# Operand loads for the last feed-forward step moved to the head of each tile and onto ScalarE's DMA queue

## The reference

```python
def _L0_attn_ref(x, Wk, bk, Wv, bv, Wq, bq):
    k = jnp.fft.fft(x @ Wk.T + bk)
    v = jnp.fft.fft(x @ Wv.T + bv)
    q = jnp.fft.fft(x @ Wq.T + bq)
    kv = jnp.cumsum(k * v, axis=1)
    queried = kv * jnp.conj(q)
    nrm = jnp.sqrt(jnp.sum(jnp.abs(queried) ** 2, axis=-1, keepdims=True))
    queried = queried / (1e-09 + nrm)
    return jnp.real(jnp.fft.ifft(queried)) / np.sqrt(d)

def _L0_ffn_ref(x, k0, k1, k2, s0, s1, s2):        # weights are booleans, +1 or -1
    h = jnp.concatenate([x, -x], axis=-1)
    h = jax.nn.relu(s0 * _conn_dense(k0, h)) * 2    # 2048 -> 4096
    h = jax.nn.relu(s1 * _conn_dense(k1, h)) * 2    # 4096 -> 4096
    return s2 * _conn_dense(k2, h)                  # 4096 -> 1024

xn = _layernorm(x)                                  # x: (4, 8192, 1024)
x = x + _L0_attn_ref(xn, ...) + _L0_ffn_ref(xn, ...)
```

## Time and profile before

| | |
|---|---|
| Time before, median of 2 runs | 4163.52 us |
| The two runs | 4025.52 and 4301.52 us |
| Profiled execution, its own time | 4029.55 us |
| Its span on the slowest core (core 7) | 4026.0 us |
| Spans of the eight cores | 4003.2 to 4026.0 us |
| Busy share of the span: PE, DVE, ACT, POOL | 91%, 28%, 28%, 17% |

### The profile page before, as it was taken

One profiled execution on the slowest core, in us unless ns is written; L12 is line 12 of the kernel. 1 busy time (PEld: TensorE's weight loads), 2 busy tenths in 40 slices (PEclk: granted clock), 3 DMA queues, 4 the chain that ended last, 5 costly groups with the idle time before them and its releaser, 6 DMA issues.

```text
span 4026.0 us, 43761 instructions; the slowest of 8 cores (4003.2 to 4026.0 us)
## 1 busy us (share of the span) xinstructions
PE 3647.3 (91%) x16512; PEld 1590.1 (39%) x16512; DVE 1118.4 (28%) x1586; ACT 1131.1 (28%) x1504; POOL 698.7 (17%) x843
## 2 busy tenths in 40 slices
PE   4667896998994999999899999999989999999998
PEld 1323332333332444444344344444434444444443
DVE  0044446876860112011111201111121111112112
ACT  4744542555562110311311131031112103112110
POOL 0022224554640001001000100100010020011001
PEclk9778898999997999999999999999999999999999
DMA  4143346334315345234344523433343442344344
GB/s 84 21 105 84 86 98 105 68 82 97 63 48 162 136 153 178 88 147 149 115 155 154 170 94 148 148 122 148 147 157 115 151 152 105 148 148 134 126 157 136
DMA packets 331229, 491.52 MB, mean 122 GB/s; under 512 B 217360, under 2 KB 219408, under 8 KB 297232
## 3 DMA queue, kind: packets, MB, share of 16 engines
q0 software_dynamic: 97904, 377.53, 28.5%
q1 hardware_dynamic: 223504, 82.90, 8.9%
q10 hardware_dynamic: 9616, 28.32, 2.0%
HBM read 276.87 MB, written 58.72 MB: 83 GB/s over the span
## 4 chain that ended last, share of the span: by engine, by line
PE 82%; DMA 5%; DVE 4%; issue 3%; ACT 3%; SPq 2%; POOL 0%; DVEq 0%; ACTq 0%; POOLq 0%
PE pd L966 44%; PE pd L661 13%; PE pd L922 11%; PE pd L1037 10%; PE pd L666 2%; PE pd L297 2%; DMA xn_f<-xn_dram 1%; SPq L533 1%; DMA w2ring<-k2u 1%; SPq L900 1%; DMA wtmp<-Wk 1%; DVE bx_t L1066 1%; PE pd L504 1%; DVE xn_t L482 1%; DMA xn_dram<-xn_t 1%
## 5 line engine op out<-in xcount | busy, mean ns | idle before, releaser
L966 PE MATMUL pd<-r_t,w1r 128*128 128x512 bf16 x8192 | 1769.4, 379 | 7.8 <-ACT r_t L936 7.8
L966 PEld LDWEIGHTS pd<-r_t,w1r 128*128 128x128 bf16 x8192 | 801.0, 98 | 976.2 <-issue 11.5
L984 DVE TENSOR_SCALAR w1r<-w1r 128x4096 bf16<-128x4096 bf16 x232 | 284.7, 1227 | 1810.3 <-DMA w1r<-w1s 1810.3
L922 PE MATMUL pd<-xn_f,K0d_t 128*128 128x512 bf16 x2048 | 459.1, 388 | 109.9 <-DVE bx_t L1070 55.9
L992 ACT ACTIVATE r_t<-pd,s_scales 128x512 bf16<-128x512 f32 x256 | 175.9, 687 | 1112.5 <-PE pd L966 1111.8
L979 POOL DMA_DIRECT2D w1r<-w1s x232 | 123.7, 533 | 2083.6 <-PE pd L966 2053.4
L1037 PE MATMUL pd<-w2ring,r_t 128*128 128x512 bf16 x2048 | 445.5, 379 | 14.3 <-ACT r_t L992 7.8
L922 PEld LDWEIGHTS pd<-xn_f,K0d_t 128*128 128x128 bf16 x2048 | 203.7, 100 | 365.4 <-issue 134.6
L1037 PEld LDWEIGHTS pd<-w2ring,r_t 128*128 128x128 bf16 x2048 | 198.8, 98 | 261.0 <-issue 25.7
L936 ACT ACT_TABLE_LOAD x64 | 82.1, 1283 | 588.0 <-PE pd L922 519.4
L1053 DVE TENSOR_SCALAR w2ring<-w2ring 128x1024 bf16<-128x1024 bf16 x224 | 95.8, 428 | 436.9 <-DMA w2ring<-k2u 436.9
(11 more groups left out here) (151 smaller groups left out, 2484.4 us busy)
## 6 DMA issues: line engine op xcount, KB each, us to landing
w1r<-w1s POOLq DMA_DIRECT2D x256, 1024.0 KB, 4.6
w2ring<-k2u POOLq DMA_DIRECT2D x256, 256.0 KB, 2.7
conv_t<-k0u POOLq DMA_DIRECT2D x64, 256.0 KB, 3.9
w1s<-k1u SPq DMA_DIRECT2D x32, 512.0 KB, 5.9
bx_t<-x_own SPq DMA_DIRECT2D x32, 512.0 KB, 4.7
out<-bx_t ACTq DMA_DIRECT2D x32, 512.0 KB, 3.3
x_t<-x_extra POOLq DMA_DIRECT2D x8, 1024.0 KB, 10.4
k0s<-conv_o SPq DMA_DIRECT2D x32, 256.0 KB, 2.6
```

Source lines behind the costliest of these rows:

```text
L922: inst = te.matmul(reg.ap, K0d_t[:, dk * F0 + m * 128: dk * F0 + (m + 1) * 128], xn_f[fb][:, dk * TST:(dk + 1) * TST], start=(dk == 0), st ...
L966: inst = te.matmul(reg.ap, w1ring[c % 3][:, k * 128:(k + 1) * 128], r0_t[:, k * TST:(k + 1) * TST], start=(k == 0), stop=(k == NF0 - 1))
L984: lambda: v.tensor_scalar(w1ring[c % 3][:], w1ring[c % 3][:], 2.0, -1.0, op0=OP.mult, op1=OP.add))
```

## The change

In `emit_compute_b` the four loads of `part_t` and the four of `bx_t` are emitted at the head of the tile, ahead of the first layer, and not between the second and third layers. The `bx_t` loads go from SP's list to ScalarE's. Buffers, sizes and numbers of transfers stay as they were. The edit in the loop of part A leaves out an `if` whose two branches were the same.

```diff
@@ -807,10 +807,7 @@
-        if it < NST:
-            emit_next_xload()
-        else:
-            emit_next_xload()
+        emit_next_xload()
@@ -907,6 +904,17 @@
     def emit_compute_b(j, fkeys):
         fb = j % 2
+        for tci in range(NTC):
+            @block.scalar
+            def _(sc, j=j, tci=tci):
+                dstep(sc, "act", s_pr[tci], [f"partial_dram{tci}"], [f"bpart{tci}"],
+                      lambda: sc.dma_start(
+                          part_t[tci][:],
+                          partial_dram.ap()[j * TST + tci * 128: j * TST + (tci + 1) * 128, :]))
+                dstep(sc, "act", s_bx[tci], [], [f"bx{tci}"],
+                      lambda: sc.dma_start(
+                          bx_t[tci][:],
+                          x_own.ap()[j * TST + tci * 128: j * TST + (tci + 1) * 128, :]))
@@ -994,21 +1002,6 @@
-        for tci in range(NTC):
-            @block.scalar
-            def _(sc, j=j, tci=tci):
-                dstep(sc, "act", s_pr[tci], [f"partial_dram{tci}"], [f"bpart{tci}"],
-                      ...
-
-            @block.sync
-            def _(sync, j=j, tci=tci):
-                dstep(sync, "sp", s_bx[tci], [], [f"bx{tci}"],
-                      ...
```

More of the change, by code:

```diff
@@ L996, in emit_compute_b @@
         r1keys = [f"r1_{c}" for c in range(NF1)]
-        for tci in range(NTC):
-            @block.scalar
-            def _(sc, j=j, tci=tci):
-                dstep(sc, "act", s_pr[tci], [f"partial_dram{tci}"], [f"bpart{tci}"],
-                      lambda: sc.dma_start(
-                          part_t[tci][:],
-                          partial_dram.ap()[j * TST + tci * 128: j * TST + (tci + 1) * 128, :]))
-            @block.sync
-            def _(sync, j=j, tci=tci):
-                dstep(sync, "sp", s_bx[tci], [], [f"bx{tci}"],
-                      lambda: sync.dma_start(
-                          bx_t[tci][:],
-                          x_own.ap()[j * TST + tci * 128: j * TST + (tci + 1) * 128, :]))
         for c in range(4):
```

## The result

| | |
|---|---|
| Ratio to before | 1.0033, 95% interval 1.002 to 1.0045 |
| Profiled execution's span, slowest core | 4035.7 us (4019.2 to 4035.7) |
| Median of 17 runs | 4040.95 us (4034.34 to 4615.12) |
| Kernel before, all 16 runs | 4080.82 us (4022.62 to 4663.73) |

The change costs 0.33%, some 13 us, where 7 us were forecast.

A forecast was written before the change was run, and what follows sets the result against it. The prediction took TensorE, busy 91% of the span, to bound the kernel. It summed 4029.55 + 5 (start) + 2 (seven borders) + 0 = 4036.5 us, with a range of 4018 to 4175.

The forecast's parts named there:

- the upper bound of a gain: All of TensorE's waits for w2ring together, 6.4 us, as the most the change could win; taken as 0.
- The term for the start of part B: Eight loads, 3 MB, issued at about 1217 beside the transposes that TensorE waits for: a cost of 5 us.
- sharing about half and half: Start of part B: moved loads partly ahead of the transposes, partly in the slack after 1254; 5 us, between 0 and 9.
- The upper bound of 9 us: Start of part B: the cost if 3.1 MB go wholly ahead of the transposes at 349 GB/s.
- The term for the seven borders: ScalarE's eight issues and four store-landing waits ahead of the first relu: 2 us for seven borders, kept between 0 and 20.
- the supply by issue time: Borders: eight issues behind the fourth store end at S + 6.6, the first region comes free at S + 8.6: cost 0.
- S: The start of a tile's first matmul, from which the prediction counts times at a border.
- two supply times: When ScalarE frees the first region at a border: S + 8.6 by issue time; S + 8.6 to S + 12.0 by landing.
- the need: Borders: when TensorE's fifth chain wants the first region, at S + 8.85 to S + 9.75 at three borders.
- stores would land less hindered: Borders: all bx_t loads now stand behind the fourth store's issue; against it, up to 1 MB of part_t loads runs there.
- The slower one: Rival: ScalarE held up at each border, 7 x 2.9 = 20 us, clock 14, start 9: 4073 us; chance 0.13.
- The faster one: Rival: w2ring and the stores relieved, the start of part B hides its 3 MB: 4023 us; chance 0.1.

The follow-up runs named there:

- e4: Against the kernel before, only bx_t's four loads at the head on ScalarE, part_t's at the old place: ratio 1.000 (0.9957 to 1.0042).
- e5: The changed kernel with a fifth bx_t buffer, so the fourth load no longer waits for the store issued just before: ratio to before 1.0037 (1.0014 to 1.006).
- e13: Against the kernel before, only bx_t's four loads at the head on ScalarE, plus a fifth bx_t buffer: ratio 1.0018 (1.0001 to 1.0034).
- e7: The kernel before with eight extra ScalarE issues of 64 columns (0.2 MB) at the start of part B: start wait 51.7 us, against 50.7 before.

## Why the prediction was right or wrong

- What bounds the kernel, and where the change acts. Right. No row outside the two places changed by more than the cores differ, and the issue time taken off SP's list (1.98 us on the first tile) and off ScalarE's behind the second layer (1.79 us) brought nothing. The w2ring waits, the upper bound of a gain, went from 4.2 to 3.8.
- The term for the start of part B, 5 us. Too small: 7.2. The step of the prediction that failed here is "sharing about half and half". I let part of the 3.1 MB fit into the half-empty stretch after 1254. But half empty is not free: what ran in that stretch was the tail of the transposes themselves, and they had come to be issued late. On core 7 SP's third transpose took until 1246.87 to be issued, and from 1252.73 on SP issued one every 1.27 us, the eighth at 1255.28. With 3.1 MB more in flight all of them come later (on core 6 after, the eighth is issued at 1262.06), and the engines stay full until then. The runs with 1, 2.1, 3.1 and 6.3 MB lie near one line of 2.5 us per MB. The upper bound of 9 us, all bytes ahead, was the nearer of the two ends.
- The term for the seven borders, 2 us. Too small: 5.5. The step that failed here is the supply by issue time, "3.8 us: 1612.4, or S + 6.6", which gave cost 0. Its two supply times were the right pair, and the square of e4, e5 and e13 shows that the later one counts. The choice between them was also right: issue time decides in the changed kernel. Its size was off. I put ScalarE free of issues at S + 6.6 by adding the mean issue times of two quiet places; core 6 shows S + 7.1 to 7.5 at five borders and S + 8.1 and 8.2 at the two where one issue takes 1.6 or 1.95 us. The eight issues take 4.9 us in the mean of 56 borders and not 3.8, and from the last issue's end to TensorE's next matmul it is 2.3 us and not 1.97, so that on core 6 the first region comes at S + 9.4 to S + 10.6 and not at S + 8.6. The distance to the need was only 0.3 us at the tightest border, so each such excess became a wait. A slack that small can't be booked as cost 0.
- That stores would land less hindered, as all loads stand behind them on one queue. They did: the fourth store landed 3.6 us after its issue in the mean, against 5.3 before. In the prediction the Trainium skill ("DMA: Bandwidth & Descriptors", queues, rings and completion order) stood beside this with its turns between queues. The runs are in line with that, and don't show it: the loads also start later than before, when most stores have landed. What the prediction made of the rule, that the border costs 0, did not come true.
- The other rule that the prediction took from the Trainium skill, that one hardware issue at a time locks the descriptor generator ("Perfetto Trace Analysis", DMA Instruction — HWDGE). Its consequence for the sum, none, held. In the changed kernel ScalarE's first `bx_t` issue at the start takes 2.12 us instead of 0.5, beside SP's transposes; e7, with eight such issues and few bytes, lost 1.0 us. Whether that is the lock was not tried. The 17 long issues at the borders are something else, since no other engine issues a DMA beside them.
- The rivals. The slower one had the right place and the right sign of it (the first relu later than about S + 9), and gave 4073; but it was priced by landings as at the sixth border, 2.9 us each, and in this order landings are not what holds ScalarE, and the longest wait at any of the 56 borders is 2.5 us. The faster one fell: no wait it counted on went away.
- The overall verdict, within 2%, held. The loss was larger than 0 beyond the interval, and about twice the 7 us forecast, because both terms were too small: 5 for 7.2 at the start, and 2 for 5.5 at the borders. That each was inside its stated bounds (0 to 9, 0 to 20) helps little, since the bounds were wide and the working chose the cheap side of both.

## What to carry to other kernels

A DMA issue cost its engine about half a microsecond here, and now and then two, so a row of loads "issued early" is not free when the engine that issues them is also the one that frees PSUM: put them behind the first group of work that someone waits for, not ahead of it. Where a phase begins with DMA engines at full load, every MB in flight with the first operand delays it (here by 2.3 to 2.9 us, on ScalarE's queue as on POOL's); load first what is wanted first. And release a PSUM region behind its last reader, then check what else stands in the list of the engine that frees the next one: here the stores took back 25 of 45 us until they were moved.

## What was not expected of the hardware

- Plain DMA issues on ScalarE's queue usually took 0.40 to 0.47 us, and at 17 of the 56 borders one took 1.2 to 2.5 us, with no landing to wait for and no issue of another engine beside it. It was mostly the first `bx_t` load behind the four stores, at the second, fourth and sixth borders. The cause stays open.
- The same 512 KB store, the fourth of a tile, landed after 3.6 us in the mean with 3 MB of loads issued behind it on its own queue, and after 7.3 us with the same loads issued sooner on another.
- A stand of TensorE of 1.6 us left the granted clock at its upper level (1.00), one of 8 us brought it to the lower (0.50), and behind one of 3.6 us a stretch of 2 us reads 0.57. At the lower level the first chain of a tile is 2 us longer.
